# A two-attention transformer layer on one core: the last unit's values issued behind the next group's first scores, and maxima 56 pieces ahead in the second attention

## What is computed

```python
x = x + attn_a(layernorm(x))   # 32 heads of 16, all keys, rotary positions
x = x + ffn(layernorm(x))      # one matrix product with its low-rank part folded in
x = x + attn_b(layernorm(x))   # 32 heads of 16, causal, with a linear position bias
x = x + ffn(layernorm(x))
# attention: probs = softmax(q @ k.T * scale); out = probs @ v, then @ Wo
```

## Time and profile before

| | |
|---|---|
| median of 3 executions | 1765.24 us (1760.79 to 1771.05) |
| the profiled execution | 1764.37 us; its span 1762.2 us, 2.2 us lie around it |
| PE, DVE, ACT, POOL busy share | 93%, 80%, 55%, 12% |
| attention a, groups 1 to 14 | one group each 42.5 us |
| attention b, groups 1 to 13 | one group each 29.3 us |

### The profile page before, as it was taken

How to read it: one execution, slowest core, us unless ns; L and a number is a source line. 1 busy time by engine, 2 the same in 40 slices (tenths; PEclk the granted TensorE clock), 3 DMA queues, 4 the chain that set the end, 5 groups by cost and what they waited for, 6 DMA issues and landing times. The chain is left out here.

```text
span 1762.2 us, 32974 instructions
## 1 busy us (share of the span) xinstructions
PE 1643.6 (93%) x13040; PEld 848.8 (48%) x13040; DVE 1402.5 (80%) x2959; ACT 969.0 (55%) x1095; POOL 213.8 (12%) x272
## 2 busy tenths in 40 slices
PE   6898999999999999999999999999999999999888
PEld 3554333333333333333344777655545555554667
DVE  3776799999999999999548364568898888899675
ACT  2433277777777777777821112126666666667210
POOL 3332200000000000000013021020101000003331
PEclk9999699999999999999999999989999999999999
DMA  7766433333333333331140433773645454542211
GB/s 212 224 169 197 91 57 61 75 62 61 61 60 62 62 61 65 61 59 59 57 157 24 143 102 112 213 158 58 112 82 92 77 93 78 95 77 87 88 69 72
DMA packets 116801, 167.58 MB, mean 95 GB/s; under 512 B 20772, under 2 KB 58036, under 8 KB 116532
## 3 DMA queue, kind: packets, MB, share of 16 engines
q1 hardware_dynamic: 115176, 160.99, 39.8%
q0 software_dynamic: 1472, 4.49, 1.3%
HBM read 100.41 MB, written 64.50 MB: 94 GB/s over the span
## 5 line engine op out<-in xcount | busy, mean ns | idle before, releaser
L358 DVE TENSOR_REDUCE mxp<-ps_m 128x1 f32<-128x512 f32 x1280 | 798.7, 684 | 69.5 <-PE ps_m L324 64.2
L686 ACT ACTIVATE a_p<-a_ps_s 128x1024 f32<-128x1024 f32 x512 | 522.6, 1025 | 149.1 <-PE a_ps_s L607 132.4
L686 ACT ACTIVATE b_p<-b_ps_s 128x1024 f32<-128x1024 f32 (+1 forms) x320 | 294.9, 939 | 158.5 <-PE b_ps_s L607 155.2
L355 DVE CUSTOM_DVE_ANT_0 ps_m<-ps_m,b_masks 128x128 f32<-128x128 f32 (+3 forms) x512 | 240.0, 517 | 43.6 <-PE ps_m L324 39.5
L324 PE MATMUL ps_m<-slot_qk 62*128 62x512 f32 (+3 forms) x624 | 230.9, 451 | 12.2 <-DVE mxp L358 8.9
L324 PE MATMUL ps_m<-a_slot_qk 62*128 62x512 f32 x640 | 237.6, 449 | 0.8
L607 PE MATMUL a_ps_s<-a_slot_qk 64*128 64x512 f32 x640 | 231.6, 442 | 1.7 <-DMA a_slot_qk<-cturned 0.5
L631 PE MATMUL a_ps_o<-a_p,a_slot_v 128*32 128x256 f32 x2560 | 205.6, 390 | 9.9 <-ACT a_p L686 5.4
L607 PEld LDWEIGHTS a_ps_s<-a_slot_qk 64*128 64x128 f32 x640 | 96.2, 185 | 129.4 <-issue 122.7
L281 POOL CAST cparts<-negm 128x16 fp32r<-128x16 f32 x64 | 12.6, 197 | 1119.3 <-DVE negm L364 1119.3
L607 PE MATMUL a_ps_s<-slot_qk 64*128 64x512 f32 x384 | 136.4, 455 | 0.7
(11 more groups left out here) (217 smaller groups left out, 2420.5 us busy)
## 6 DMA issues: line engine op xcount, KB each, us to landing
va_groups<-w_o SPq DMA_DIRECT2D x16, 512.0 KB, 3.6
ka_parts<-pa_parts SPq DMA_DIRECT2D x16, 512.0 KB, 3.9
qa_parts<-pa_parts SPq DMA_DIRECT2D x32, 256.0 KB, 3.7
kb_parts<-slot_memory SPq DMA_DIRECT2D x16, 512.0 KB, 3.9
qb_parts<-slot_memory SPq DMA_DIRECT2D x32, 256.0 KB, 3.4
vb_groups<-w_proj SPq DMA_DIRECT2D x16, 512.0 KB, 3.4
a_slot_qk<-qa_parts SPq DMA_DIRECT2D x60, 128.0 KB, 4.3
a_slot_qk<-ka_parts SPq DMA_DIRECT2D x48, 128.0 KB, 6.6
```

Source lines behind the costliest of these rows:

```text
L355: dve.tensor_tensor_reduce(from_, from_, mask_of_query[:, CHUNK - keys:], 1.0, LOWEST, ALU.add, ALU.max, accum_out=to).then_inc(piece_take ...
L358: dve.tensor_reduce(to, from_, AX.X, ALU.max).then_inc(piece_taken, 1)
L686: act.activation(p_sb[:, (2 * u + pair) % NP, :, off:CHUNK], ps_s[:, 2 * pair:2 * pair + 2, off:CHUNK], ACT.Exp, scale=scale).then_inc(exp ...
```

## The change

Two things. First, the last unit's values of a group (u = NU - 1) go behind the scores of the next group's first unit, as those of every other unit do; ACT's copy of the finished half goes behind the exponentials of that unit. After the last group both come alone. Second, in attention b `AHEAD` is 56: pieces run one group and 8 pieces ahead. `BEGUN` stays at 48 for b, so that group 0 issues 56 pieces between its units, and group 14 only the 40 that are left.

```diff
-    AHEAD = 48 if causal else 44
+    AHEAD = 56 if causal else 44
...
+    BEGUN = early.pieces if AT_ONCE else AHEAD
+    before_unit_of_first = [2 * round((NPC + AHEAD - BEGUN) * sum(columns[:u]) / sum(columns) / 2)
+                            for u in range(NU + 1)]
...
+                def values_behind(s, u, part):
+
+                    if u:
+                        values(s, s % SLOTS, u - 1, part)
+                    elif s:
+                        values(s - 1, (s - 1) % SLOTS, NU - 1, part)
+
...
                     for u in range(NU):
                         lo, hi = AHEAD + before_unit[u], AHEAD + before_unit[u + 1]
+                        if s == 0:
+                            lo, hi = BEGUN + before_unit_of_first[u], BEGUN + before_unit_of_first[u + 1]
                         cut = lo + PAIR * ((hi - lo + PAIR) // (2 * PAIR))
+
                         half_unit(s, j, u, 0, lo, cut)
-                        if u:
-                            values(s, j, u - 1, 0)
+                        values_behind(s, u, 0)
                         half_unit(s, j, u, 1, cut, hi)
-                        if u:
-                            values(s, j, u - 1, 1)
-                    values(s, j, NU - 1, 0)
-                    values(s, j, NU - 1, 1)
+                        values_behind(s, u, 1)
...
                         if u == last_of[0] + 1:
                             copy_out(s, 0)
-                    copy_out(s, 1)
+                        if u == 0 and s:
+                            copy_out(s - 1, 1)
```

More of the change, by code:

```diff
@@ L663, in keep_clock @@
                     pe.matmul(ps_s[:, 2 * PAIR - 1, 0:columns], x[:, 0:P], x[:, 0:columns], start=True, stop=True)
-                for i in range(early.pieces, AHEAD, PAIR):
-                    ahead(0, 0, i, min(i + PAIR, AHEAD))
+                for i in range(early.pieces, BEGUN, PAIR):
+                    ahead(0, 0, i, min(i + PAIR, BEGUN))
                     keep_clock(CHUNK // 2)
@@ L669, in _ @@
                     step(s, s % SLOTS)
+                for part in range(2):
+                    values_behind(NG, 0, part)
             @block.scalar
@@ L695, in _ @@
                     step(s)
+                copy_out(NG - 1, 1)
             @block.vector
```

## The result

The change made the kernel slower: a median of 1778.95 us (8 runs, 1768.32 to 1786.11) against 1765.45 us before (8 runs, 1759.39 to 1771.05), a ratio of 1.0073 [1.0049, 1.0097]. The forecast was 1752, in a range of 1743 to 1764. The profiled execution took 1779.42 us, 15.1 more than the one before; its span is 15.0 longer.

A forecast was written before the change was run, and what follows sets the result against it. PE's beat was taken to set the time, with waits for ACT at changes of groups. -12.8 - 1.3 + 0 + 1 + 2 - 2.1 = -13.2 gave 1751.2 us for the profiled execution, 1752 for the median; range 1743 to 1764.

The forecast's parts named there:

- Attention a, -12.8: Changes of groups in a: 5.08 us become 4.23, a gain of 0.85 at each of 15, -12.8 us.
- The new order in b, -1.3: Groups 0 to 13 of b: late rows of maxima shrink a gain of 1.1 us to 0.1 each, -1.3 in all.
- AHEAD 56: Units 2 to 4 of b: DVE stands 2.6 us, PE loses 0.5 and regains it; 0, range -0.4 to +0.5 a group.
- DVE becomes the bound in b: Rival, groups of b: DVE's wait and the pieces' new places add 0.5 us a group, sum 1760; chance 0.21.
- Slack that is gone, +2: Group 2 of b: its late landing of rows, which cost 0.66 us, now costs its whole 2.6; +2 (0 to 4).
- Group 14 and group 0, +1: Ends of b: 8 more pieces in group 0, part at half clock, against 8 fewer in group 14; +1 (0 to 2).
- Last group and the end, -2.1: End of b: DVE's chain to `fin` moves up about 5 us, PE's longer wait for rows costs 1.7; -2.1 us.
- the same wait on DVE, but with landings that are late in most groups: Rival, 13 groups of b: DVE and PE stand up to 2.6 us more each; at +2 a group 1779; chance 0.05.

The follow-up runs named there:

- e1: Against the kernel before: the new order of the last unit's values in attention a only, AHEAD 48 in b; 1754.24 us, ratio 0.9937.
- e4: The whole change, with SP in b issuing the next group's rows of maxima ahead of the stores of half 1; 1750.42 us, ratio 0.9912.
- e6: As e4 (rows of maxima ahead of the stores), but with AHEAD 48 in b; 1748.4 us, ratio 0.9915.
- e5: The whole change, SP's order kept, but each half in b has its own part of cturned and its own semaphore; 1767.49 us, ratio 1.0019.
- e3: Against the kernel before: AHEAD 56 in b, with the old order of values and copies in both attentions; 1766.38 us, ratio 1.0009.
- e2: The whole change's new order of values in both attentions, but AHEAD left at 48 in b; 1776.67 us, ratio 1.0077.
- e8: As e2, but PE repeats a piece three times, without use, ahead of unit 3's scores to fill its wait; 1782.62 us, ratio 1.0109.
- e10: As e6, but DVE's two reciprocals at the end of group 13 are parted by 12 pieces; 1752.01 us, ratio 0.9914.
- e9: As e4, but group 0's 8 extra pieces all stand in its last two units; 1753.48 us, ratio 0.9925.

## Why the prediction was wrong

By its own steps, in the order of the sum:

- *Attention a, -12.8.* Right. The change of groups takes 4.23, groups take 41.67 on average with the one of 42.8 left out, the block is 11.6 us shorter, and e1 measures 11.1 for it alone.
- *The new order in b, -1.3.* The marks were right to 0.2 us, and the core of the argument too: SP's queue makes the rows late and uses up the gain. But PE "would reach unit 3 at +8.5" was wrong. With the rows in time, e4 shows what it can reach: +9.38. The turnings and the wider pieces of `AHEAD` 56 now stand in units 1 and 2, ahead of that mark, which I had counted only against DVE: from the new group's first values to unit 3 e4 needs 4.82 us, where before it was 4.13. `AHEAD` 48 is no way round it: in e6, with the turning still in unit 0, the copy stands at +4.41 and unit 3 at +9.27. So there was a gain of 0.3 to 0.4 to lose, not 1.1, and PE's own wait was 0.1 to 0.2, not 1.
- *AHEAD 56: "in unit 3 PE then loses some 0.5 us to DVE, and gets about as much back in unit 4 ... I take 0".* **This is the step that failed**, and with it its bounds of -0.4 to +0.5. The stand of DVE was foreseen at 2.6 us and measured 1.80. The loss was foreseen too. The "gets it back" was not true: from unit 3 to the next unit 8 the changed kernel needs 20.51 us, e4 with the same places of pieces 19.62. That is 0.85 to 0.89 that never comes back, and e5, which takes only DVE's wait away, measures 0.85. I had reckoned DVE's slack over a whole group (3.25 us idle). But it lies unevenly: from 1484.28 on DVE works for 9 us with a single gap, of 0.29, and its idle time later in the group doesn't give back what PE lost in these (that this is why is argued from the trace; that the wait costs 0.85 is shown). The rival "DVE becomes the bound in b", which had 0.21, is this mechanism as far as its price of +0.5 a group goes; the price was 0.85, and e3 shows that it is not the pieces' places that bring it, but the wait.
- *Slack that is gone, +2.* Too small by about 8 us. In the change the late groups cost up to 4 us over an ordinary one, where the forecast had the bare wait of 2.6, once. Two things were missed. The rows can be late by SP's issue as well as by their landing: the four stores ahead of them took 2.96 at 1263.65 where others take 1.84. The trace before had this, in a group with slack enough to hide it:

```profile
1410.94 2.75 SPq L536 DMA_DIRECT2D ob_sums<-out_b_sums  x4
1413.74 1.30 SPq L295 DMA_DIRECT2D slot_qk<-cturned  x2
```

The copy of that group stands at 1409.72, so the rows are issued 4.02 us behind it and not 3.09. And low clock follows many of the waits. First the rows: behind the wait of 1.19 at 1269.27 the granted clock is 0.53 for 7 us, and behind that of 2.06 in e2 it is 0.50. The Trainium skill, "TensorE: Matmul & The Clock Gate", section "HAM oscillation — how this bites in real kernels", says that a PE which waits for a DMA in every round of a loop starts each round at the low clock; the forecast cited it for the last group alone. The traces agree in part, in the middle of b as well: the waits of 1.19 and 1.42 were followed by 6.8 us of low clock each, though they are shorter than the 3 to 5 us of the page's case, and that of 1.38 at 1333.22 was followed by none. I had left it out there because 0.95 idle had kept the full clock and I saw only one wait longer than that coming.
- *Group 14 and group 0, +1.* Off by 5.6: 4 us for 8 pieces in group 0 at an unchanged clock (e1 against e3), and about 3.5 that go with the longer low clock, whose cause is open. I had priced a piece by the last group, 0.13 us at the full clock; in group 0 it cost 0.5. That PE's half speed there is the reason is likely, but no run shows it.
- *Last group and the end, -2.1.* Right: -1.6. PE waits 1.68 us for the rows and `fin` starts 3.7 us sooner after the last copy.

Forecast and result are some 28 us apart: 11.8 in b's ordinary groups, 7.8 in late rows and the clock behind them, 5.6 in group 0, 1.2 in a, 1.1 before it, 0.8 in the rest. (The forecast's own range, 1744 to 1760, is narrower than its bounds of a and b added up, 1740 to 1763; the result lies far outside either.) The rival on the other side ("the same wait on DVE, but with landings that are late in most groups") had the right place but asked for the wrong trigger: it took no later landing than the ordinary one.

## What to carry to other kernels

When an instruction is moved behind other work, follow what its end releases, through every in-order queue, down to the next single-buffered tile: here a copy 1.9 us later made small urgent rows late behind bulk stores that nobody waits for, and issuing the rows ahead of the stores turned a loss of 0.7% into a gain of 0.9%. An engine's idle time over a group says nothing about whether it can make up a stand in one place: look at how dense its work is in the stretch right behind it. Where a change makes PE wait again and again, price a fall of the clock as well as the wait: in the change and in e2 it followed ten of twelve waits of 1.19 us or more, and in other runs some shorter ones.

## What the hardware did that I had not expected

SP's issue of the same four stores mostly takes 1.8 to 2.1 us and sometimes 2.3 to 3.4. In e2 those of half 1 took 2.75, 3.13, 2.70, 2.97 and 2.85 in five groups, at 1194.78, 1257.93, 1322.21, 1537.33 and 1601.82, and just these five, the last group aside, have waits of PE for the rows of 1.56 to 2.06. The rows themselves landed in the ordinary time: 1261.10 to 1263.72 is 2.62. In e6 the issue is as slow at times, and nobody waits, as its timeline shows:

```profile
1506.67 1.26 SPq L301 DMA_DIRECT2D o_qk<-cturned  x2
...
1509.20 3.27 SPq L542 DMA_DIRECT2D ob_sums<-out_b_sums  x4
...
1512.86 0.50 PE L615 MATMUL b_ps_s<-o_qk 64*128 64x512 f32 x1
```

The slow issues are not scattered: those of half 1 take 2.65 to 3.44 us in groups 2 and 4 of all ten kernels with the new order in b, and 2.26 to 3.32 in groups 11 and 13 of nine of them; before, all four had 1.83, and groups 7 and 9 had 2.75 and 2.35. Why an issue takes longer at these places was not tried.

The length of an idle stretch of PE does not tell by itself whether the clock falls. In b of the changed kernel and of e2, no fall followed nine waits for rows of 0.77 to 1.05, one of 1.38 and one of 1.56; waits of 1.19, 1.42 and 1.49 and seven of 1.63 to 2.06 were followed by 3.4 to 13.7 us at 1.2 GHz. But in e8 13.7 us followed a wait of 0.97, in e10 3.4 us one of 0.94, in e1 10.2 us one of 0.96 for DVE, in e3 10.2 us one of 0.63, and in e9 the clock fell with no wait at all. What else decides it, no run here shows.
